# Attention heads of a 24-stage kernel: two heads' rows on the two partition halves, one max instruction for two banks, exps of two banks and one in turn

## The reference

```python
# L2_attn: 16 heads of 8, RoPE on q and k, softmax over all 2048 keys
scores = jnp.einsum('bhqd,bhkd->bhqk', q, k) / jnp.sqrt(HEAD_DIM)
attn = jax.nn.softmax(scores, axis=-1)
ctx = jnp.einsum('bhqk,bhkd->bhqd', attn, v)
# L3_attn: the same with another RoPE and a causal mask
# L3_ffn (run twice): the same without RoPE; q is scaled by a sigmoid per token and head
scale = jax.nn.sigmoid(jnp.einsum('bhsd,hd->bhs', q, scale_w)) * 2.0
```

## Time and profile before

| | |
|---|---|
| median of 3 runs | 4514.57 us (4512.73 to 4515.37) |
| profiled execution | 4526.3 us, its span 4524.5 us |
| TensorE busy | 3962.3 us, 88% of the span |
| VectorE busy | 3194.4 us, 71% |
| ScalarE busy | 2199.4 us, 49% |
| GpSimd busy | 97.5 us, 2% |
| mean granted TensorE clock | 0.907 |
| HBM | 68.91 MB read, 14.70 MB written |

### The profile page before, as it was taken

How to read it: one execution, slowest core, us unless ns; L and a number is a source line. 1 busy time by engine, 2 the same in 40 slices (tenths; PEclk the granted TensorE clock), 3 DMA queues, 4 the chain that set the end, 5 groups by cost and what they waited for, 6 DMA issues and landing times.

```text
span 4524.5 us, 59451 instructions
## 1 busy us (share of the span) xinstructions
PE 3962.3 (88%) x22108; PEld 1619.8 (36%) x22108; DVE 3194.4 (71%) x6776; ACT 2199.4 (49%) x2694; POOL 97.5 (2%) x59
## 2 busy tenths in 40 slices
PE   5989797599999984999999986399894899999986
PEld 3756655122222232222222363133232232222253
DVE  5256255688888835888888548486774888888546
ACT  2222321166666651466666721156473266666721
POOL 0000000200000001000000001100001000000000
PEclk8889898599999995799999988599897699999988
DMA  0011500100000002000000000100001000000000
GB/s 23 4 43 25 116 1 6 70 1 22 2 22 2 2 6 77 12 2 22 22 2 1 20 1 0 70 2 23 22 2 47 24 2 22 11 13 2 1 19 10
DMA packets 37282, 87.42 MB, mean 19 GB/s; under 512 B 7080, under 2 KB 31432, under 8 KB 32200
## 3 DMA queue, kind: packets, MB, share of 16 engines
q1 hardware_dynamic: 36856, 82.09, 5.7%
q10 hardware_dynamic: 144, 1.53, 0.1%
HBM read 68.91 MB, written 14.70 MB: 18 GB/s over the span
## 4 chain that ended last, share of the span: by engine, by line
PE 75%; DVE 16%; DMA 3%; ACT 2%; SPq 2%; issue 2%; POOL 0%; ACTq 0%; DVEq 0%
PE ps L1767 18%; PE ps L1752 18%; PE ps L1732 15%; DVE pm L1817 8%; PE ps L945 3%; PE ps L948 3%; PE ps L2058 3%; PE ps L1024 3%; PE ps L2034 3%; SPq L1308 2%; DMA m_dram<-mt 1%; PE ps L1458 1%; DVE XN L289 1%; PE ps L1208 1%; PE ps L744 1%
## 5 line engine op out<-in xcount | busy, mean ns | idle before, releaser
L1817 DVE TENSOR_REDUCE pm<-ps 128x1 f32<-128x512 f32 (+2 forms) x3712 | 2258.9, 669 | 453.6 <-PE ps L1732 413.8
L1793 ACT ACTIVATE arena<-ps 128x1024 f32<-128x1024 f32 x1728 | 1684.8, 1022 | 791.5 <-PE ps L1752 788.1
L1732 PE MATMUL ps<-arena 72*128 72x512 bf16 (+2 forms) x3712 | 1453.5, 398 | 154.3 <-DMA arena<-parts_dram 127.6
L1752 PE MATMUL ps<-arena 75*128 75x512 bf16 (+1 forms) x3712 | 1385.7, 382 | 57.1 <-DMA arena<-m_dram 52.1
L1767 PE MATMUL ps<-arena,VA 128*16 128x512 f32 (+2 forms) x7424 | 965.7, 592 | 0.0
L1752 PEld LDWEIGHTS ps<-arena 75*128 75x128 bf16 x3712 | 357.1, 98 | 1098.6 <-issue 771.5
L1732 PEld LDWEIGHTS ps<-arena 72*128 72x128 bf16 x3712 | 368.6, 100 | 672.9 <-DVE pm L1817 338.0
L1767 PEld LDWEIGHTS ps<-arena,VA 128*16 128x16 f32 x7424 | 122.9, 94 | 310.8 <-issue 299.8
L976 DVE TENSOR_TENSOR arena<-EV,ps 128x512 f32<-128x512 f32 x128 | 87.8, 686 | 125.4 <-PE ps L948 120.8
L964 ACT ACTIVATE EV<-ps 128x512 f32<-128x512 f32 x128 | 76.2, 597 | 203.5 <-PE ps L945 203.5
L945 PE MATMUL ps<-XNT,arena 128*128 128x512 f32 x304 | 160.9, 612 | 2.3 <-DVE arena L1251 1.5
(11 more groups left out here) (263 smaller groups left out, 2795.6 us busy)
## 6 DMA issues: line engine op xcount, KB each, us to landing
arena<-parts_dram SPq DMA_DIRECT2D x72, 384.0 KB
parts_dram<-parts SPq DMA_DIRECT2D x32, 384.0 KB, 3.4
arena<-k_dram SPq DMA_DIRECT2D x20, 528.0 KB, 11.2
arena<-parts_dram SPq DMA_DIRECT2D x96, 96.0 KB
parts<-k_dram SPq DMA_DIRECT2D x8, 528.0 KB, 6.4
arena<-in_w SPq DMA_DIRECT2D x4, 1024.0 KB, 6.2
VA<-k_dram SPq DMA_DIRECT2D x4, 528.0 KB, 7.4
arena<-in_w12T SPq DMA_DIRECT2D x1, 2048.0 KB, 13.2
```

The lines of the kernel that those rows point to most:

```text
L1732: ins = e.matmul(bank[:, 0:w], QP[0:KR, g % 2, hh, i * P:(i + 1) * P], KP[0:KR, g % 2, hh, kc * CH:kc * CH + w], start=True, stop=not diag)
L1752: ins = e.matmul(bank[:, off:CH], KP[0:KM, g % 2, hh, j * P:(j + 1) * P], QP[0:KM, g % 2, hh, q * CH + off:(q + 1) * CH], start=True, stop ...
L1793: e.activation(self.PB[:, pb, :, :], c.bank(2 * k, 2).rearrange("p (a t) -> p a t", a=2), ACT.Exp, scale=self.scale).then_inc(self.exped.s ...
L1817: e.tensor_reduce(c.pm[:, u % 2, hh * TPC + qt, kc:kc + 1], self.slot_bank(slot)[:, 0:w], AX, ALU.max).then_inc(self.emptied.sem, 1)
```

## The change

- Only 6 of the 9 products of parts are kept (`Q_PARTS`, `K_PARTS`): `KR` = 48, `KM` = 51.
- The heads are ordered by parity. The rows of the even heads lie on partitions 0 to 50, those of the odd ones on 64 to 114, for all 16 heads at once (eight pairs). Every product of scores or maxima is now issued as two, one per half, into two banks.
- A maxima step fills two banks of a slot; there are two slots (banks 4 and 5, 6 and 7). One `tensor_reduce` covers both banks, 2 x 512 columns: 32 in a noncausal unit.
- Scores use banks 0 to 2. Tile t (one head, one key tile) goes to bank t mod 3; exps cover tiles 0 and 1, then 2, then 3 and 4, then 5. The values add into bank 3 after every key tile. The exps' target is a ring of 15 tiles instead of 8 pairs.
- All gathers are issued in `Prepare`: 12 DMAs per chunk, over all 16 heads. `Heads` issues none. The rows of ones come by two DMAs from a new input instead of two memsets on GpSimd.
- The split of the maxima moves from VectorE to GpSimd (five steps), the copy of their transpose from VectorE to ScalarE, their rows are read back by two DMAs instead of one, and their transpose follows after four ticks instead of three. `LEAD` is 9 of the new, shorter steps.
- `Prepare` keeps two chunks of rows in a ring instead of all tokens; `Rope` and `Temper` work on them.

```diff
-TERMS = SPLIT * SPLIT
+PAIRS = HEADS // 2
+Q_PARTS = (0, 0, 0, 1, 1, 2)
+K_PARTS = (0, 1, 2, 0, 1, 0)
+TERMS = len(Q_PARTS)
...
-GATHERS = 2 * SPLIT
-def gather_rows(e, c, g, t0, n, marks):
...
+GATHERS = 12
+def gather_rows(e, c, t0, n, marks):
+    for w, rows in enumerate(packed(c)):
+        for par in range(2):
+            for term, part, step in ((0, 0, w), (3, 1 - w, w), (5, 2 * (1 - w), 0)):
+                n_terms = {0: 3, 3: 2, 5: 1}[term]
+                src = bass.AP(tensor=c.parts_dram.tensor,
+                              offset=(w * SPLIT + part) * P * T + par * (P // 2) * T + t0,
+                              ap=[[step * P * T, n_terms], [PAIRS * T, HD], [T, PAIRS], [1, n]])
+                first = par * (P // 2) + term * HD
+                e.dma_start(rows[first:first + n_terms * HD, :, t0:t0 + n], src).then_inc(marks.sem, 16)
...
 class HeadsPlan:
-    LEAD = 8
+    LEAD = 9
...
+    def score_pair(self, u, j, pp, last):
+        q = self.units[u][1]
+        off = max(0, (j - TPC * q) * P) if self.causal else 0
+        first = self.tiles
+        self.tiles += 2
+        self.tile_off += [off, off]
+        self.steps.append(("scores", u, j, pp, first))
+        while len(self.exp_of) < self.tiles:
+            t = len(self.exp_of)
+            n = 2 if t % 3 == 0 else 1
+            if t + n > self.tiles:
+                if not last:
+                    break
+                n = 1
+            self.exp_of += [self.exps] * n
+            self.steps.append(("exp", t, n, self.exps))
+            self.exps += 1
...
+                    self.score_pair(u, j, pp, u == len(units) - 1 and j == n_keys - 1 and pp == 1)
+                    for _ in range(n):
+                        self.run(pending.pop(0))
                     self.tick()
+                waiting.append((u, j, first, j == n_keys - 1))
+                if len(waiting) > 1:
+                    self.values(*waiting.pop(0))
...
     def tensor(self, e):
...
             if what == "max":
-                ins = e.matmul(bank[:, 0:w], QP[0:KR, g % 2, hh, i * P:(i + 1) * P],
-                               KP[0:KR, g % 2, hh, kc * CH:kc * CH + w], start=True, stop=not diag)
+                for par in range(2):
+                    rows = slice(64 * par, 64 * par + KR)
+                    ins = e.matmul(c.bank(b + par)[:, 0:w], QR[rows, 2 * g + pp, i * P:(i + 1) * P],
+                                   KT[rows, 2 * g + pp, kc * CH:kc * CH + w], start=True, stop=not diag)
...
             elif what == "scores":
-                    if n > 1:
-                        e.wait_ge(*self.exped[n - 2])
+                if t > 1:
+                    e.wait_ge(*self.exped[plan.exp_of[t - 2]])
+                for par in range(2):
+                    rows = slice(64 * par, 64 * par + KM)
+                    ins = e.matmul(c.bank((t + par) % 3)[:, off:CH], KT[rows, 2 * g + pp, j * P:(j + 1) * P],
+                                   QR[rows, 2 * g + pp, q * CH + off:(q + 1) * CH], start=True, stop=not diag)
...
     def scalar(self, e):
...
+                if n == 2 and offs[0] == offs[1]:
+                    e.activation(self.PB[:, s:s + 2, offs[0]:CH],
+                                 c.bank(0, 2).rearrange("p (a t) -> p a t", a=2)[:, :, offs[0]:CH], ACT.Exp,
+                                 scale=self.scale).then_inc(self.exped.sem, 1)
...
     def vector(self, e):
...
-                e.tensor_reduce(c.pm[:, u % 2, hh * TPC + qt, kc:kc + 1], self.slot_bank(slot)[:, 0:w], AX,
-                                ALU.max).then_inc(self.emptied.sem, 1)
+                banks = c.bank(self.slot_banks(slot), 2).rearrange("p (a t) -> p a t", a=2)
+                e.wait_ge(*self.filled[slot])
+                e.tensor_reduce(pm[:, pp, :, qt], banks[:, :, 0:w], AX, ALU.max).then_inc(self.emptied_v.sem, 1)
```

More of the change, by code:

```diff
@@ L1591, in tick, with keys, values @@
                 self.run(item[1])
-    def batches(self, k):
-        n = TPC * (k + 1) if self.causal else NT
-        return [(j, j + 1) for j in range(0, n, 2)]
-    def offsets(self, k, pair):
-        return [max(0, (j - TPC * k) * P) if self.causal else 0 for j in pair]
-    def values(self, items, u, last):
-        for jj in range(2):
-            self.steps.append(("values", u, jj, items, last))
-            yield
+    def keys(self, k):
+        return TPC * (k + 1) if self.causal else NT
+    def score_pair(self, u, j, pp, last):
[15 more added lines that the diff above has]
+            self.exps += 1
+    def values(self, u, j, first, last):
+        self.steps.append(("values", u, j, first, last))
         if last:
+            self.last_tile[u] = first + 3
             self.steps.append(("empty", u))
-            self.later.append([3, ("out", u)])
+            self.later.append([4, ("out", u)])
     def lay_out(self):
         units = self.units
-        self.steps.append(("gather", 1))
         for step in self.maxima(0):
@@ L1615, in lay_out @@
         for _, k in units:
-            starts.append(starts[-1] + len(self.batches(k)) * GH)
-        pending, reached, queued, total, clock, waiting = [], 0, [], 0, 0, None
+            starts.append(starts[-1] + 2 * self.keys(k))
+        pending, reached, queued, total, clock = [], 0, [], 0, 0
+        waiting = []
         for u, (g, k) in enumerate(units):
-            if u % NC == 0 and 1 <= g < NG - 1:
-                self.steps.append(("gather", g + 1))
-            todo = self.batches(k)
-            for b, pair in enumerate(todo):
-                items = []
-                for hh in range(GH):
+            n_keys = self.keys(k)
+            for j in range(n_keys):
+                first = self.tiles
+                for pp in range(2):
                     while reached < min(u + 2, len(units) - 1):
@@ L1631, in lay_out @@
                     clock += 1
[L1632 to L1648 removed]
+                    self.score_pair(u, j, pp, u == len(units) - 1 and j == n_keys - 1 and pp == 1)
+                    for _ in range(n):
+                        self.run(pending.pop(0))
+                    self.tick()
+                waiting.append((u, j, first, j == n_keys - 1))
+                if len(waiting) > 1:
+                    self.values(*waiting.pop(0))
+        for item in waiting:
+            self.values(*item)
         self.tick(True)
         self.tick(True)
+        rows = set(self.rows_slot.values())
+        for slot in range(self.slots):
+            self.turned.append((slot in rows, sum(r < slot for r in rows)))
 class Heads(Stage):
[L1656 removed]
+    PBS = 15
     def __init__(self, chip, before, causal):
@@ L1734, in tensor @@
                 if diag:
[L1735 removed]
+                    for par in range(2):
+                        ins = e.matmul(c.bank(b + par)[:, w - P:w], c.IDB[:, :], c.MQB[:, :], start=False, stop=True)
                 ins.then_inc(self.filled.sem, 1)
@@ L1769, in tensor @@
+                e.wait_ge(*self.exped[plan.exp_of[first + 3]])
+                if j == 0:
+                    e.wait_ge(*(self.copied[u - 1] if u else self.zeroed[0]))
+                for hh in range(GH):
+                    ins = e.matmul(c.bank(3)[32 * hh:32 * hh + VW, off:CH], c.VA[:, j, GH * g + hh, :],
+                                   self.PB[:, (first + hh) % self.PBS, off:CH], start=j == 0, stop=last,
                                    tile_position=(0, 32 * hh))
-                    if jj == 1:
-                        ins.then_inc(self.valued.sem, 1)
+                ins.then_inc(self.valued.sem, 1)
@@ L1837, in vector @@
+            elif step[0] == "rows":
                 _, u, slot = step
```

382 lines of the change are left out of this document (177 added, 205 removed).

## The result

The changed kernel takes **4993.03 us** (median of 4 runs, 4986.49 to 4998.65) against 4514.97 for the kernel before: a ratio of 1.105, 95% interval 1.103 to 1.108. It is slower, as predicted; the predicted 4882 us is 111 us too low and inside the range of 4620 to 5130. The profiled execution took 4998.65 us.

What follows compares the result with a forecast made beforehand. The open round trip between scores and exps was taken to bound the loop, gathers each stage's start: 4526.3 + 175 - 46 + 239 = 4894 us profiled, median 11.7 lower, 4882 us, 8% slower; range 4620 to 5130.

Steps and rivals of the forecast that it cites:

- gathers, four stages: Start of each stage: first product waits for all 48 transfers, 100 us against 40.5, +60 per stage, +239 for four.
- loops of the three full stages: Noncausal loops: 3.03 us per key tile against 2.83, 800 us against 741.6, +58 per stage, +175 for three.
- causal loop: Causal stage: whole key tiles 3.03 us, diagonal ones 2.63, 474 us in all against 502.
- stall ahead of the causal stage: Wait before the causal stretch, 18 us above normal, goes because maxima's rows no longer queue behind the next group's gather.
- rest: Small parts: first unit's maxima -2 us per stage, maxima split on GpSimd +1, second row transfer +0.7; together 0.
- closed round: Scores and exps with three banks: three times in six tiles the exp-to-scores-to-exp trip of 0.58 us lies open.
- forecast's own range: Whole kernel: 4760 to 5000 us, with loop 2.9 to 3.15, gathers +45 to +75; chance 0.67.
- halves run together: TensorE: two products on the array's two halves go out as a pair, taken at 0.23 us, second starting 0.03 later.
- Rival 1: TensorE pairs: the halves don't run beside each other, 3.60 us per key tile, 5370 us; chance 0.07.
- Rival 4: Loop: the exps' round doesn't hold and VectorE sets the pace, 4221 us, faster; chance 0.06.
- rival 2: TensorE's clock falls with less work and gaps; at 1.2 GHz half of the time, 5530 us; chance 0.08.
- Rival 3: Stage starts: the gathers spread over more engines, +0 to +16 us per stage, 4645 to 4710 us; chance 0.12.

Runs made afterwards that it cites:

- same-half run: Changed kernel with both products of each pair reading the rows of the first half, so they can't run side by side: 6830.86 us, wide scatter.
- single exps: Changed kernel with every exp over one bank instead of two and one in turn: 4676.22 us, ratio 1.035 to the kernel before.
- four banks: Changed kernel with four score banks in two pairs, all exps over two banks, maxima in three banks with 512-column reduces: 4748.81 us, ratio 1.051.
- Two experiments: Changed kernel with the causal stage's off-diagonal score pairs issued twice, 5000.47 us; or its off-diagonal pairs of products for the maxima instead, 5013.98 us.

## Why the prediction was right, point by point

```
term, us                           predicted    measured
gathers, four stages                  +239        +290
loops of the three full stages        +175        +132
causal loop                            -28         +74
stall ahead of the causal stage        -18         -17
rest                                     0          -7
sum against the span                  +368        +472
```

The direction and the two main causes, the waits for the gathers and the closed round, were right. That the time also lies in the forecast's own range of 4760 to 5000, by 7 us, is partly luck: the full loops, priced 43 us too high, took back some of the 153 us that the causal loop and the gathers were priced too low.

- **The halves run together** at 0.22 us per pair: right. Rival 1 is refuted by the same-half run.
- **The closed round sets the pace**: right in kind, and shown from two sides, by single exps (-317) and four banks (-244). Its size was 0.49 us (0.06 + 0.43), not 0.58: the 0.14 from the earlier trace rows was one release, and the pair's second product starts with the first. With 0.49 my own count of six steps gives 4 x 1.51 + 1.09 + 1.52 = 8.65 us, not 9.10: 2.88 per key tile, and most of the loop runs at that pace (8.66). The six steps shown above take 8.75 because one release took 0.15. Rival 4 (VectorE sets the pace) did not happen: VectorE was busy 83% in the loop and waited before most reduces. It happened in the kernel with four banks, at 91%, though with reduces over one bank and at 2.78 us per key tile, not at rival 4's price. What the Trainium skill warns of ("TensorEngine Tiling (Array Packing)", PSUM Bottleneck) is seen there and not in the changed kernel.
- **The full loops.** +132 instead of +175 hides two errors. Between first and last units a unit costs only 47.5 against 46.5 us. The loss sits in the last two: +11.0 and +27.7 us of the +47 in the first stage. I had spread one pitch over all 16 units and had not read that the old kernel sped up to 31.8 us in its last one, when the maxima were done; the new one can't. At the round's 2.92 us it would take 2.92 x 16 = 46.7 (an estimate, the pace being that of units with maxima). The other 13 us are put down to rival 2, the clock, to which I gave a chance of its own and no share in the forecast: with pairs issued twice and the clock up, the last units took 9 to 12 us less.
- **The causal loop** is the step that failed: -28 predicted, +74 measured. "Whole ones cost 3.03 ... on the diagonal 2.63" prices a key tile by its own scores and exps. That holds for units of 16 key tiles (48.8, 48.4 and 49.6 us; my prices give 47.4), but a short unit also has to make the maxima of the longer one that follows. My prices give 11.0 us for a unit of 4 key tiles and 23.1 for one of 8. Apart from the last unit of each length, these took 21 to 41 and 28 to 37. With reduces of a quarter of the columns they take 12.7, 12.7 and 29.2, and 25 to 26: 49 of the 102 us missed, some of it through the clock that rose with it. In the kernel before the same units were long too (31.8 us for the first of 8 key tiles), so what would have told me was the copy times of the old loop, which no group of rows shows. The other 53 us are not pinned down. The granted clock (0.79 against 0.92 before in the same stage) has a part: the same code took 17 us less in an execution at 0.84. Two experiments did not isolate it.
- **The stall** of 18 us ahead of the stage went, as predicted: 31.75 to 15.04 us from the first maxima product to the first scores.
- **The gathers** are a mis-sized term: 113 us against 100. With 7.8 us for the rest as before (2.36 MB at 73 GB/s are 32.3 us and not 32.7, so 8.2; it changes little), my count of 2176 pieces of 1 KB on the fullest engine leaves 105 us, 48 ns each and not 42. That the shape of the transfers and not the bytes sets the wait is shown: the same bytes took 73 us with 8 rows per transfer and 43 with 48. Rival 3 is out. Which engines carried which piece no row shows. The Trainium skill ("DMA: Bandwidth & Descriptors", Why a DMA increments its semaphore by 16 and not by 1) gives the number of engines as the largest up to 16 that divides the slowest dimension of both sides. The shares agree with it. Where gathers alone ran they were 0.18 to 0.19 with 3, 2 and 8 mixed, 0.39 to 0.50 with 8 alone and 1.13 with 48.

## What to carry to other kernels

When products get cheaper, count the banks between producer and consumer before the engines: three banks with exps of two left no exp to run beside the round trip, and the loop ran at the speed of that round. Read the old kernel's units one by one, first, last and short ones too, because the mean hides where one engine's work is done for a later unit. And lay out data for transfers so that the outermost dimension is long and the transfers are few: the same bytes took 113, 73 or 43 us.

## What the runs showed of the hardware

- With less work on TensorE the granted clock fell in places where it had been 1.00: 0.50 from 1718 to 1762 us, with TensorE busy 33.5 of 44 us. Issuing score pairs twice in the last units raised it to 0.88 from 1680 to 1762 us (0.57 without), and the three loops took 27 us less. But a window of the same-half run, in its slowest execution, had 0.58 at 95% busy.
- The same heads code took 576.6 us in the causal stage at a mean granted clock of 0.79 and 559.8 at 0.84.
- Two products on two halves start together and end together: 0.39 us for both at the high level, 0.60 at the low one.
- SyncE issued transfers of 64 KB in 8 rows 0.71 us apart, so that 96 of them took 68.6 us; 56 of 96 KB in 48 rows went out 0.48 us apart, and those on few engines 2.2 us apart.
- From DRAM to SBUF in pieces of 1 KB, with gathers alone in the window, shares of 0.18 to 0.19 of the engines moved 58 to 61 GB/s, 0.39 to 0.50 moved 94 to 97 and 1.13 moved 195.
